# Key norms of layer 0: sums of squares dealt to partitions by a transfer inside SBUF, in place of five identity matmuls per pass

## The reference, cut to what matters

```python
def _ln(x, w, b):
    mu = jnp.mean(x, axis=-1, keepdims=True)
    var = jnp.mean(jnp.square(x - mu), axis=-1, keepdims=True)
    return (x - mu) * jax.lax.rsqrt(var + EPS) * w + b
...
k = _ln(k, kln_w, kln_b)                          # 256 own tokens
kx = _ln(kx.reshape(b, sc, g, d), kxln_w, kxln_b)  # 1601 context tokens
scores = jnp.einsum('bsghd,btgd->bghst', q, k) * scale
```

## Time and profile before

| what | value |
|---|---|
| time, median of 3 | 1788.65 us (1786.4 to 1791.87) |
| span of the profiled execution | 1787.7 us |
| lead-in, before pair 0 is scored | to about 90 us |
| attention of layer 0 | to about 1240 us |
| mixture of experts and layer 1 | the remaining 548 us |
| PE busy | 1631.5 us, 91% |
| DVE busy | 1474.9 us, 83% |
| ACT busy | 1386.3 us, 78% |
| POOL busy | 1367.9 us, 77% |

### The profile page before, as it was taken

The page is one execution under the profiler, slowest core; times in us unless marked ns, Lnnn a source line. Parts: engine busy times, 40 slices in busy tenths (PEclk is TensorE's granted clock), DMA queues, the critical chain, the costliest instruction groups (busy, mean ns, idle before and its releaser), DMA issues. The chain is left out here.

```text
span 1787.7 us, 44278 instructions
## 1 busy us (share of the span) xinstructions
PE 1631.5 (91%) x16245; PEld 1038.3 (58%) x16438; DVE 1474.9 (83%) x3476; ACT 1386.3 (78%) x2365; POOL 1367.9 (77%) x1171
## 2 busy tenths in 40 slices
PE   3389999999999999999999999997898999999997
PEld 1256776777767767777777777765454333333332
DVE  8889999999999989999999999998896765645422
ACT  4287887888878777887887888775234999999996
POOL 3557787887878888888888888887897998979500
PEclk8599999999999999999999999999899999999999
DMA  4268999999899979999999999998523222222100
GB/s 168 93 130 180 184 187 193 198 194 190 189 199 184 200 150 198 191 231 184 195 195 192 217 213 190 194 186 160 171 42 110 41 44 75 43 37 43 31 14 13
DMA packets 603176, 261.42 MB, mean 146 GB/s; under 512 B 568784, under 2 KB 575952, under 8 KB 601552
## 3 DMA queue, kind: packets, MB, share of 16 engines
q1 hardware_dynamic: 602960, 258.57, 70.1%
HBM read 99.15 MB, written 17.28 MB: 65 GB/s over the span
## 5 line engine op out<-in xcount | busy, mean ns | idle before, releaser
L1800 PE MATMUL pv<-PT,VV 128*128 128x256 bf16 (+1 forms) x2880 | 340.9, 275 | 9.2 <-DMA PT<-PB 9.2
L1780 PE MATMUL score<-KK,QT 128*128 128x512 bf16 (+2 forms) x1795 | 315.6, 318 | 32.6 <-DVE mxp L1249 24.3
L2370 POOL TENSOR_TENSOR l_rr<-l_rr,mhalf 128x32 f32<-128x32 f32 (+1 forms) x60 | 332.8, 5546 | 5.0
L1521 ACT ACTIVATE PB<-S,rsum 128x1024 bf16<-128x1024 f32 (+1 forms) x256 | 246.2, 988 | 105.3 <-DVE rsum L1281 101.1
L1800 PEld LDWEIGHTS pv<-PT,VV 128*128 128x128 bf16 (+1 forms) x2880 | 280.7, 99 | 76.4 <-issue 35.2
L1272 DVE SCALAR_TENSOR_TENSOR PB<-S,rsum,PB 128x1024 bf16<-128x1024 f32 (+1 forms) x256 | 318.7, 1246 | 2.7 <-ACT PB L1521 2.6
L1780 PEld LDWEIGHTS score<-KK,QT 128*128 128x128 bf16 x1920 | 159.9, 98 | 164.5 <-DVE mxp L1249 32.3
L1511 ACT ACTIVATE S<-S,nmx 128x1601 f32<-128x1601 f32 x128 | 209.7, 1638 | 28.3 <-DVE nmx L1263 27.8
L2636 ACT ACTIVATE P<-score 128x1024 f32<-128x1024 f32 x196 | 199.4, 1063 | 12.7 <-PE score L2728 6.0
L1076 POOL TENSOR_SCALAR S<-S,rsum 128x256 f32<-128x256 f32 x128 | 122.0, 954 | 86.1 <-DVE rsum L1281 86.1
L2748 PE MATMUL pv<-P,V 128*9 128x256 f32 (+1 forms) x2288 | 153.9, 384 | 3.8 <-DVE pv L2174 2.4
(11 more groups left out here) (275 smaller groups left out, 3686.7 us busy)
## 6 DMA issues: line engine op xcount, KB each, us to landing
x<-rs_d SPq DMA_DIRECT2D x16, 936.0 KB, 7.6
rsb<-rs_d SPq DMA_DIRECT2D x16, 936.0 KB, 6.0
wsb<-w_split SPq DMA_DIRECT2D x46, 256.0 KB, 4.7
wsb<-w_split SPq DMA_DIRECT2D x23, 512.0 KB, 5.2
wpr<-in_wprojT SPq DMA_DIRECT2D x23, 512.0 KB, 3.9
context_d<-stage SPq DMA_DIRECT2D x16, 400.2 KB, 3.7
l_ctx<-context_d SPq DMA_DIRECT2D x4, 1601.0 KB, 8.1
rawh<-in_w_all SPq DMA_DIRECT2D x12, 512.0 KB, 5.6
```

The source lines that it names most:

```text
L1521: e.activation(m.PB[n % 2][:, 2 * a:a + b], m.S32[n % 2][:, a:b], ACT.Copy, scale=m.rsum[n % 2][:, 1:2]).then_inc(s["p_hi"], 1)
L1780: i = e.matmul(m.score[:, at:at + b - a], qt[:, kind, qp, q * P:(q + 1) * P], kk[:, kp, a:b], start=(k == 0), stop=(k == 2))
L1800: i = e.matmul(m.pv[:, at:at + 256], vv[0:rows, v, t, :], m.PT[k % 2][0:rows, turned(c, a), :], start=(c == first and r == 0), stop=(c == ...
L2370: e.tensor_tensor(rr, rr, m.mhalf[0:rows, 0:NH1], ALU.pow).then_inc(s["l1_rr"], 1)
```

## The change

The four products of `squares` are laid out so that each band of 32 partitions holds 480 sums. ScalarE adds eps as it copies them out. SP then deals them out with one DMA inside SBUF: from 4 partitions with 480 values to 128 partitions with 15 values (`turn_sums`). GpSimd raises 128 by 15 values to the power, after the split of query tile 4 it + 1 and no longer before it. `row_out` writes `rr` itself, 128 rows of 15 values (60 bytes), where it wrote 16 rows of 117 (468 bytes). Steps 3, 4, 6 and 7 are gone; the slot of step 3 is left empty, so the bank of `V2` now waits for `Q1` to be read out. Two small tiles move to another place in SBUF.

```diff
-SQG, SQT = 4, 4
-SQW = (KC + SQG * SQT - 1) // (SQG * SQT)
-SQN = SQG * SQT
-RSC = SQN * SQW
+SQG = 4
+SQC = (KC + P - 1) // P
+SQW = P * SQC // SQG
+RSC = KC + 15
...
-SLOTS = (("Q0",), ("K0",), ("K1",), ("TQ0",), ("K2",), ("K3",), ("Q1",), ("SS",), ("V0",), ("ST",), ("V1",), ("TQ1",),
-         ("V2",), ("RS", "V3"), ("PR",))
+SLOTS = (("Q0",), ("K0",), ("K1",), ("TQ0",), ("K2",), ("K3",), ("Q1",), ("SS",), ("V0",), (), ("V1",), ("TQ1",), ("V2",),
+         ("V3",), ("PR",))
...
+    def turn_sums(it):
+        if not it < NGB:
+            return
+        e.wait_ge(s["sums_out"], it + 1)
+        if it:
+            e.wait_ge(s["kr_pow"], it)
+        e.dma_start(m.ssc[:, :], m.sqs[0:SQG * R:R, :].rearrange("j (r c) -> j r c", c=SQC)).then_inc(s["sums_in"], 16)
+
     def row_out(it):
         if not it < NGB:
             return
-        e.wait_ge(s["rst_out"], it + 1)
+        e.wait_ge(s["kr_pow"], it + 1)
         if it >= 2:
             e.wait_ge(s[f"rs_in{it % 2}"], 16 * (it // 2))
-        e.dma_start(m.rs_d[it % 2], m.rsr[0:SQN, 0:SQW]).then_inc(s["rs_row"], 16)
+        e.dma_start(m.rs_d[it % 2], m.rr[:, :]).then_inc(s["rs_row"], 16)
...
+        if it >= 0:
+            turn_sums(it + 1)
         turn_p(4 * it + 1, 0)
         row_out(it + 1)
...
-        e.wait_ge(s["ssq_out"], it + 1)
+        e.wait_ge(s["sums_in"], 16 * (it + 1))
         if it:
-            e.wait_ge(s["pa_full"], made(it - 1, "RS"))
-        else:
-            e.wait_ge(s["p_pad"], 1)
-        e.tensor_tensor(m.rr[0:SQW, 0:SQN], m.ssc[0:SQW, :], m.mhalf[0:SQW, 0:SQN], ALU.pow).then_inc(s["kr_pow"], 1)
+            e.wait_ge(s["rs_row"], 16 * it)
+        e.tensor_tensor(m.rr[:, :], m.ssc[:, :], m.mhalf[:, 0:SQC], ALU.pow).then_inc(s["kr_pow"], 1)
...
+        split_self(4 * it + 1)
         key_norm(it + 1)
         if it == -1:
             pool_round_end(e, m, s, 5)
-        split_self(4 * it + 1)
...
-            e.wait_ge(s["pa_full"], made(it - 1, "ST"))
-        e.copy(m.sqs[:, :], bank_of(m, "SS")[:, 0:SQT * SQW]).then_inc(s["sums_out"], 1)
+            e.wait_ge(s["sums_in"], 16 * it)
+        e.activation(m.sqs[:, :], bank_of(m, "SS")[:, 0:SQW], ACT.Copy, bias=D * EPS5).then_inc(s["sums_out"], 1)
...
         squares(it + 1)
         times_v(2 * it - 1, 1)
         values(it + 1, 0)
-        turn_squares(it + 1)
         scores(4 * it + 2, 1)
         values(it + 1, 1)
         turn_queries(it + 1, 1)
         values(it + 1, 2)
-        turn_norms(it + 1)
         values(it + 1, 3)
```

More of the change, by code:

```diff
@@ L138, in allocate @@
     m.ones = sb(whole, "ones", [P, R], F32)
+    m.wg = sb(whole, "wg", [P, IC, NE], F32)
+    m.brow = sb(whole, "brow", [P, NE], F32)
     m.kb = sb(whole, "kb", [P, 2], BF16)
@@ L183, in allocate @@
             m.wsb = sb(c, "wsb", [P, 2 * IC * WCOLS], BF16)
[L184 to L185 removed]
+            m.sq = sb(c, "sq", [P, SQG * SQW], F32)
+            m.sqs = sb(c, "sqs", [P, SQW], F32)
             m.kn = [sb(c, f"kn{i}", [P, 512], F32) for i in range(2)]
@@ L894, in wait_bank @@
         it, at = it - 1, at + len(SLOTS)
-    if SLOTS[at] == ("PR",) and 0 <= it < LAG:
+    if not SLOTS[at] or SLOTS[at] == ("PR",) and 0 <= it < LAG:
         at -= 3
@@ L959, in row_in @@
             e.wait_ge(s["mm"], 12 * (it - 1))
-        e.dma_start(m.rsb[it % 2], m.rs_d[it % 2].rearrange("t k -> (t k)").partition_broadcast(P)).then_inc(
+        e.dma_start(m.rsb[it % 2], m.rs_d[it % 2].rearrange("t k -> (t k)")[0:RSC].partition_broadcast(P)).then_inc(
             s[f"rs_in{it % 2}"], 16)
@@ L980, in sp_attention @@
             sp_store_inputs(e, m, s, 4)
+            turn_sums(0)
             sp_store_inputs(e, m, s, 5)
@@ L1206, in query_full @@
                         ALU.add).then_inc(s["q_t32"], 1)
-    def squares_out(it):
-        if not it < NGB:
-            return
-        e.wait_ge(s["pa_full"], made(it, "ST"))
-        if it:
-            e.wait_ge(s["kr_pow"], it)
-        sums = bank_of(m, "ST")[0:SQW, :].rearrange("p (t g r) -> p g t r", t=SQT, g=SQG)[:, :, :, 0]
-        e.tensor_scalar(m.ssc[0:SQW, :].rearrange("p (g t) -> p g t", g=SQG), sums, D * EPS5, None,
-                        ALU.add).then_inc(s["ssq_out"], 1)
     def projected(i):
@@ L1525, in act_attention @@
         if it == 0:
-            e.wait_ge(s["p_pad"], 4)
+            e.wait_ge(s["p_pad"], 3)
             e.wait_ge(s["w_lo_dve"], 16)
@@ L1655, in squares @@
         if it == 0:
-            e.wait_ge(s["p_pad"], 2)
-        w = SQT * SQW
+            e.wait_ge(s["p_pad"], 1)
         for j in range(SQG):
-            r = e.matmul(bank[j * R:(j + 1) * R, 0:w], m.ones[:, :], m.sq[:, j * w:(j + 1) * w], start=True, stop=True,
-                         skip_group_check=True)
-        r.then_inc(s["pa_full"], 1)
-    def turn_squares(it):
-        if not it < NGB:
-            return
-        bank = bank_of(m, "ST")
-        wait_bank(e, s, it, "ST")
-        e.wait_ge(s["sums_out"], it + 1)
-        for t in range(SQT):
-            r = e.transpose(bank[0:SQW, t * P:(t + 1) * P], m.sqs[:, t * SQW:(t + 1) * SQW], m.ident[:, :])
+            r = e.matmul(bank[j * R:(j + 1) * R, 0:SQW], m.ones[:, :], m.sq[:, j * SQW:(j + 1) * SQW], start=True,
+                         stop=True, skip_group_check=True)
         r.then_inc(s["pa_full"], 1)
@@ L1739, in turn_queries @@
         r.then_inc(s["pa_full"], 1)
-    def turn_norms(it):
-        if not it < NGB:
-            return
-        bank = bank_of(m, "RS")
-        wait_bank(e, s, it, "RS")
-        e.wait_ge(s["kr_pow"], it + 1)
-        e.transpose(bank[0:R, RS0:RS0 + SQW], m.rr[0:SQW, :], m.ident[0:SQW, 0:SQW]).then_inc(s["pa_full"], 1)
     def project(i):
```

38 lines of the change are left out of this document (9 added, 29 removed).

## The result

| | before | changed |
|---|---|---|
| time, median | 1787.53 us (1784.03 to 1791.87) | 1824.59 us (1821.39 to 1830.24) |
| ratio, with its 95% interval | | 1.0206 [1.0176, 1.0235] |
| span of the profiled execution | 1787.7 us | 1828.1 us |

The change costs 37 us; the interval of the ratio lies wholly above 1, from 1.8% to 2.4%. I had forecast a gain of 7, and 1824.6 lies outside the range of 1765 to 1799. The profile of the changed kernel is of its slowest execution (1830.2 us), so the two profiles differ by 40 us and not by 37.

What follows compares the result with a forecast made beforehand. The prediction took a loop through PE and DVE to bound early passes and PE alone late ones. From 1787.7 us it summed -6.6 (early), -2 (ACT's copy) and +1.5 (late) to 1780.6, median 1781.5, range 1765 to 1799.

Steps and rivals of the forecast that it cites:

- What bounds the kernel, and what PE gets back: Early passes set by a loop through PE and DVE, late ones by PE alone; PE saves 24 us over 31 passes.
- The 0.78 us: PE's work saved per pass: 0.70 from turning the sums, 0.11 from turning the factors, less 0.03 for wider `squares`.
- the 0.6: Gain taken for each of eleven early passes, between DVE's 0.17 and PE's 0.78 us; -6.6 us together.
- the nothing of the sum: Late passes, where gains and losses nearly cancel: +1.5 us taken for the sixteen.
- The new chain: From ACT's copy to `row_out`: transfer lands after 5.5 us, issue at 8.3 against 6.5, row 1.2 us late.
- What a late row costs: Delay less the slack of DVE's factors and PE's transposition: covered in early passes, +1.5 us over sixteen late ones.
- the row becomes the bound: Rival: row 2.5 us late, late passes lose some 1.3 us on average, about 1802 us; chance 0.2.
- GpSimd is free for it: In the chain: the split goes first and fills GpSimd's 2.09 us idle time; no cost counted for its wait.
- GpSimd becomes the bound: Rival: GpSimd's work and waits fill 34.4 us, late passes gain only 0.4, none lost; about 1777 us, chance 0.1.
- the same two slacks: Early passes: DVE's factors and PE's transposition land 2 to 6 us before their readers, covering the row's delay.
- The lower bound of the chain: Transfer lands 3.3 us after the copy, row not later; as a rival about 1766 us, chance 0.2.
- the 0.21 for slower: Forecast's chance that the change measures slower, against 0.53 for faster and 0.26 for the same.

Runs made afterwards that it cites:

- e3: Changed kernel with the transfer sent to a tile nobody reads and the power on a constant tile, so nobody waits for it: 1779.05 us, ratio 0.9955.
- e2: Changed kernel with SP issuing the small transfer ahead of the transposition of tile 4 it, half 0, and of the weight load: 1772.2 us, ratio 0.9915.
- e11: Changed kernel with the small transfer issued ahead of the 512 KB weight load, still behind the transposition: 1814.22 us, ratio 1.0148.
- e5: Changed kernel with GpSimd working on constants without waiting, while `row_out` waits for the transfer and a second small one: 1794.66 us, ratio 1.0037.
- e4: Changed kernel with GpSimd still waiting for the transfer, but `row_out` writing a constant tile once PE finished the last values: 1823.27 us, ratio 1.0202.
- e12: Changed kernel with GpSimd waiting, the row written early from a constant tile, and two unread GpSimd instructions added behind the power: 1853.14 us, ratio 1.0368.
- e1: Changed kernel with the small transfer issued by ScalarE on its own queue right behind the copy: 1780.3 us, ratio 0.9962.
- e10: Changed kernel with the power behind `add_magnitudes` and the second `query_low`, and the row written from a constant tile, so not late: 1802.73 us, ratio 1.0085.

## Why the prediction was wrong

**What bounds the kernel, and what PE gets back.** The reading of the bounds held. The 0.78 us was counted too high: by the busy time of the fourteen late passes PE works 34.2 us a pass in e3 and 34.7 before, so some 0.5 came back. With no one waiting for the transfer (e3) passes shrink by 0.45 and 0.16 us, less than the 0.6 and near the nothing of the sum; with e2 by 0.82 and 0.37.

**The new chain.** The transfer landed where I put it in late passes. In the pass above ScalarE's copy began at 1043.45 and the power at 1048.66; over the late passes the power begins 5.3 us after the copy's end (9.06 - 3.74), and I had taken 5.5. `row_out`'s DMA landed in 1.4 us, as counted. Line L949, 660 to 1200 us:

```profile
DMA to landing us min/median/max: 1.4/1.4/3.0
```

In odd early passes the term was too small: 6.5 to 8.3 us from copy to power, since the weight load stands between. The text had put the transfer right behind the transposition everywhere. e11 prices this at 10 us.

The Trainium skill, page "DMA: Bandwidth & Descriptors", section "Anatomy of one DMA", gives about 2.0 us as the fixed cost of a DMA issued from GpSimd. The least landings of this one, issued from SP, agree with it: 2.0 to 2.7 us in ten of the fourteen late passes of the changed kernel, though a transposition stood in front, and 3.4 to 4.0 in the other four. With the weight load in front too, at 491.38, it was 4.4. What e2 takes away in the late passes lies before the issue: 2.5 us of waiting for SP, against 0.1.

**What a late row costs.** The delay was right: the row lands 1.2 us later than before in the late passes of the changed kernel (20.4 against 19.2 us after `squares`), as counted. The price was put too high: the rival "the row becomes the bound" gave 1.3 us on average for a row 2.5 us late in late passes; e5 is 2.3 us later than the kernel before and pays 0.44 a pass against it (0.60 for 2.6 us against e3), and its time of 1794.7 lies below that rival's 1802. Early passes covered it in e5, as said.

**The step that failed** is the one that put GpSimd's wait at nothing. In the forecast's own chain it reads "GpSimd is free for it, since the split of 2.1 us (1087.04 to 1089.15) now goes first and fills the 2.09 us in which it idled", and the sum has no term for it; in the rival "GpSimd becomes the bound" it reads "That is 34.4, so a late pass can gain only 0.4, but none is lost". Measured, this wait alone makes the kernel 36 us slower than before (e4, 1823.3 against 1787.4), 44 us above the same kernel without it (e3). The rival compared GpSimd's work and waits with the length of a pass. What counts is how much later than before each of its results comes, and when the first reader wants it. By the prediction's own numbers the power would end at 1088.4 + 2.7 = 1091.1, where the split had ended at 1089.15: everything behind comes 1.95 us later. The slack was 0.66 us of idle time and 1.26 us at `kn`, 1.92 in all. So in that pass even the mean used all of it up, nothing was left for the gain of 0.78, and a pass with a later landing would lose. In early passes it was 2.6 us later. The prediction listed the readers of the row and none of GpSimd's, though it had moved the wait onto that engine. And the loop feeds back: behind a late `kn` PE's scores and keys come later, and so do ScalarE and VectorE (VectorE's wait for `sq`, 5.5 us over the loop before, is 27.9 in the changed kernel) and the `PB` that SP's transpositions wait for, with the transfer behind them. e4 shows that the hold of GpSimd alone is enough for the whole loss, and e12 that GpSimd has no slack left behind it. Through which reader it is paid is shown for the passes that wait for `kn`; for the others it was not followed.

**"In the early passes the same two slacks are 2 to 6 us, so the delay is covered"** was right for the row alone (e5) and wrong for the pass, since it knew only two of three slacks: the early pass grew by 1.10 us, of which 0.48 stay in e4, where the row is early. In the changed kernel VectorE waits for the row in four of the eleven early passes, so there too the two delays meet.

**The rivals.** The lower bound of the chain, the transfer slipping past the transpositions, did not occur with the order as given; made so by hand (e2) it gives 1772.2, where the rival said 1766. The chance of 0.1 for GpSimd, at a price of no loss, follows from the step that failed; the 0.21 for slower came from the row alone.

## What to carry to other kernels

When a wait moves onto another engine, write down for each result behind it in program order how much later it comes, and compare that with the slack of its first reader; the engine's busy share says too little, since here an engine busy for 77% of the span passed on all of the time that was added to it. A small transfer costs what stands ahead of it in its queue, in each kind of pass: the same DMA, issued two instructions earlier, turned a loss of 2.1% into a gain of 0.85%. And two delays need not add, so taking away one of them need not show its price: without the late row the time stayed as it was (e4), though a late row alone cost 16 us (e5).

## What the runs showed of the hardware that I had not expected

The small DMA from 4 partitions to 128 keeps SP busy for 0.56 to 0.91 us at its issue, where `row_out` takes 0.34 (tile `ssc` and line L949 of the changed kernel, 660 to 1200 us):

```profile
L941 SPq DMA_DIRECT2D ssc<-sqs x15: 561/607/913, 680.5 to 1191.8; - x15
```

```profile
L949 SPq DMA_DIRECT2D rs_d<-rr x15: 336/338/339, 685.6 to 1197.1; - x15
```

The transpositions keep SP busy much longer, 4.47 us for the two at 1041.72, and that is what the transfer waited for.

On ScalarE's queue, with nothing ahead of it there, it took 3.9 us to land on average in the late passes, against 2.5 on SP's queue ahead of the second transposition (e2). In e1 SP had mostly issued a transposition about 0.7 us before it; which of the DMAs under way it met was not tried.

In the changed kernel PE's granted clock over 900 to 1100 us fell from 1.00 of the upper level (2.4 GHz) to 0.98: it was at the lower level (1.2 GHz) from 954.3 to 961.2 us, in the longest of the late passes, 40.25 us. That adds to this pass, but the longer passes don't need it: in e10 the clock stays at 1.00, and its late passes take 36.23 us against 35.02 before.

```profile
900.00:1100.00 200.00, 191.17 (x1780) 139.13 (x1803) 188.69 (x440) 158.10 (x289) 176.70 (x169) 1.00 0.93 195
```
